# Attention layer of a macaron block: the next input's load, statistics and normalisation in other slots, and two reorderings on VectorE and on the DMA queue

## The reference

```
def attention(x, Wq, bq, Wkv, bkv, Wo, bo):            # 16 heads of 64
    q, k, v = split(x @ Wq + bq), split(x @ Wkv + bkv)
    q, k = rope(q), rope(k)                            # rotary positions
    probs = softmax(where(causal, q @ k.T / 8, -inf))  # 512 x 512 for each head
    return concat_heads(probs @ v) @ Wo + bo
```

## Time and profile before

| | us |
|---|---|
| median of 3 runs | 2536.84 (2534.6 to 2539.08) |
| the profiled execution | 2532.82 |
| its span, first to last instruction | 2530.7 |
| TensorE busy | 2345.7 (93%) |
| VectorE busy | 1879.8 (74%) |
| GpSimd busy | 1494.7 (59%) |
| ScalarE busy | 1467.9 (58%) |
| mean granted TensorE clock | 0.977 of full |

### The profile page before, as it was taken

One profiled execution on the slowest core, in us unless ns is written; L12 is line 12 of the kernel. 1 busy time (PEld: TensorE's weight loads), 2 busy tenths in 40 slices (PEclk: granted clock), 3 DMA queues, 4 the chain that ended last, 5 costly groups with the idle time before them and its releaser, 6 DMA issues. The chain is left out here.

```text
span 2530.7 us, 54615 instructions
## 1 busy us (share of the span) xinstructions
PE 2345.7 (93%) x17368; PEld 1820.5 (72%) x17368; DVE 1879.8 (74%) x3259; ACT 1467.9 (58%) x3733; POOL 1494.7 (59%) x1268
## 2 busy tenths in 40 slices
PE   7986899799999999999999999999999969976998
PEld 5753577578878888788788788888888846743676
DVE  6751377578888888898898888998888857731576
ACT  2321244377777777777777777777777723311343
POOL 1100255478888888888787888888888802100442
PEclk9998899999999999999999999999999989997999
DMA  7359664356565566566565665665665655559443
GB/s 252 117 208 391 246 196 157 99 150 177 163 178 167 161 182 172 162 179 170 151 189 157 173 174 165 168 181 156 177 175 163 177 152 190 205 235 380 135 150 104
DMA packets 336756, 460.86 MB, mean 182 GB/s; under 512 B 63200, under 2 KB 273760, under 8 KB 332384
## 3 DMA queue, kind: packets, MB, share of 16 engines
q1 hardware_dynamic: 336480, 457.47, 58.7%
HBM read 279.09 MB, written 111.15 MB: 154 GB/s over the span
## 5 line engine op out<-in xcount | busy, mean ns | idle before, releaser
L1374 POOL TENSOR_TENSOR att_z_sb<-att_z_sb,att_cos 128x512 f32<-128x512 f32 x255 | 347.9, 1364 | 222.4 <-DMA att_zs<-att_z_sb 222.2
L1585 ACT ACTIVATE att_prob<-att_ps_s,att_nmax 128x384 f32<-128x384 f32 (+2 forms) x768 | 356.5, 479 | 117.5 <-DVE att_nmax L1471 98.3
L1471 DVE TENSOR_REDUCE att_nmax<-att_ps_s 128x2 f32<-128x768 f32 (+3 forms) x512 | 410.3, 822 | 13.2
L1377 POOL TENSOR_TENSOR att_z_sb<-att_z_sb,att_zs 128x512 f32<-128x512 f32 x255 | 361.4, 1417 | 20.0
L1375 POOL TENSOR_TENSOR att_zs<-att_zs,att_sin 128x512 f32<-128x512 f32 x255 | 362.8, 1423 | 0.0
L1468 DVE TENSOR_TENSOR att_ps_s<-att_ps_s,att_masked 128x256 f32<-128x256 f32 (+1 forms) x384 | 195.5, 509 | 86.8 <-PE att_ps_s L1707 84.3
L1719 PE MATMUL att_ps_p<-sh_ident,att_prob 128*128 128x128 f32 x1536 | 236.7, 278 | 13.6 <-DVE att_probT L1485 13.4
L1585 ACT ACTIVATE att_last<-att_ps_s,att_nmax 128x512 f32<-128x512 f32 x256 | 173.9, 684 | 92.1 <-DVE att_nmax L1471 92.1
L1707 PE MATMUL att_ps_s<-att_kT_hi,att_qT_hi 64*128 64x256 f32 (+2 forms) x1024 | 194.0, 374 | 18.1 <-ACT att_prob L1585 14.6
L1733 PE MATMUL att_ps_p<-att_probT,att_v_sb 128*64 128x384 f32 (+2 forms) x1536 | 195.0, 389 | 6.7 <-DVE att_lastT L1490 6.7
L1719 PEld LDWEIGHTS att_ps_p<-sh_ident,att_prob 128*128 128x128 f32 x1536 | 170.5, 140 | 35.8 <-DVE att_probT L1485 17.7
(11 more groups left out here) (211 smaller groups left out, 6089.5 us busy)
## 6 DMA issues: line engine op xcount, KB each, us to landing
att_zs<-att_z_sb SPq DMA_DIRECT2D x512, 128.0 KB, 2.6
last_tile_blocks<-att_last SPq DMA_DIRECT2D x128, 512.0 KB, 3.0
att_got<-last_tile_blocks SPq DMA_DIRECT2D x512, 128.0 KB, 3.0
ffn_w<-in_e_W SPq DMA_DIRECT2D x56, 1024.0 KB, 13.5
att_R<-inverse_sums SPq DMA_DIRECT2D x256, 128.0 KB, 3.4
ffn_wg<-in_e_Wg SPq DMA_DIRECT2D x24, 1024.0 KB, 14.6
x_normalised_transposed<-dis_b_xnT SPq DMA_DIRECT2D x32, 512.0 KB, 2.8
dis_b_x<-in_x SPq DMA_DIRECT2D x16, 512.0 KB, 4.0
```

Source lines behind the costliest of these rows:

```text
L1374: nc.gpsimd.tensor_tensor(z[:, m, i, :], z[:, m, i, :], cos[:], ALU.mult)
L1377: nc.gpsimd.tensor_tensor(z[:, m, i, :], z[:, m, i, :], zs[:, m, i, :], ALU.add).then_inc(sum_s[i].sem, 1)
L1471: nc.vector.tensor_reduce(nmax[:, p % 2, qt, :], ps[:, :, at:at + (qt + 1) * P], AX.X, ALU.max, negate=True)\
L1585: nc.scalar.activation(dst, src, ACT.Exp, bias=nmax[:, p % 2, qt, hh:hh + 1], accum_out=sums[:, p % 2, hh, qt:qt + 1]).then_inc(exp_s.sem, 1)
```

## The change

- The residual's load goes from slot 0 of its own input to slot 7 of the input before (input 0 still loads its own in slot 0). A name BIAS = 0 keeps POOL's bias additions in slots 1 and 2.
- The next input's load goes from slot 1 to slot 0; the statistics from slot 2 (four tiles) to slots 1 and 2 (two tiles each). Moments stay in slot 3.
- `recentre` goes from the end of slot 3 to slot 4, behind `low_part` and ahead of `result`.
- `normalise` goes from slot 4's `exps` to: tiles 0 and 1 at the end of slot 4, tile 2 ahead of `exps` 2 and tile 3 ahead of `exps` 3 of slot 5.
- In slot 5 `turn` goes from ahead of `x_low` to the end of the slot, where it stands in all others; both `x_high` now stand ahead of `exps` 0.
- In every slot VectorE's `copy_pt` 1 goes from behind `largest` 2 to ahead of it.
- In every slot SP issues `rows` ahead of `get`.

```
-    XRES, X_LOAD, X_STATS, X_MOMENTS, X_NORM, X_TURN = 0, 1, 2, 3, 4, 5
+    XRES, BIAS, X_LOAD, X_STATS, X_MOMENTS, X_NORM, X_TURN = 7, 0, 0, 1, 3, 4, 5
...
                 if t.has(p - 1):
+                    rows(j, p - 1)
                     get(j, p - 1)
-                    rows(j, p - 1)
...
-                if p == XRES:
-                    need_held(sp, xo_s, j, 2 - NP)
+                if t.first and p == 0:
                     sp.dma_start(xres[:], tiles(x_dram, j)).then_inc(xres_in.sem, 16)
+                if p == XRES and not t.last:
+                    need_held(sp, xo_s, j, 2)
+                    sp.dma_start(xres[:], tiles(x_dram, j + 1)).then_inc(xres_in.sem, 16)
...
-                if p in (XRES + 1, XRES + 2):
+                if p in (BIAS + 1, BIAS + 2):
                     for i in range(2):
-                        residual(j, 2 * (p - XRES - 1) + i)
+                        residual(j, 2 * (p - BIAS - 1) + i)
...
                 if t.has(p - 2):
                     divide(j, p - 2)
+                if t.has(p - 1):
+                    copy_pt(j, p - 1, 1)
                 if t.has(p):
                     largest(j, p, 2)
-                if t.has(p - 1):
-                    copy_pt(j, p - 1, 1)
                 if t.has(p - 2):
                     low_part(j, p - 2)
-                if p == X_STATS and not t.last:
-                    statistics(j + 1, range(TT))
+                if p in (X_STATS, X_STATS + 1) and not t.last:
+                    statistics(j + 1, range(2 * (p - X_STATS), 2 * (p - X_STATS) + 2))
                 if p == X_MOMENTS and not t.last:
                     moments(j + 1)
+                if p == X_NORM and not t.last:
+                    recentre(j + 1)
...
                 if turning:
-                    turn(j, p - 1)
                     x_low(j + 1)
                 if t.output():
                     result(j, p - OUT0)
                 if t.has(p + 1):
                     query_low(j, p + 1)
-                if t.has(p - 1) and not turning:
+                if t.has(p - 1):
                     turn(j, p - 1)
-                if p == X_MOMENTS and not t.last:
-                    recentre(j + 1)
...
-                if norm:
-                    normalise(j + 1, (0,))
+                if turning:
+                    normalise(j + 1, (2,))
                 if t.has(p):
                     exps(j, p, 2)
-                if norm:
-                    normalise(j + 1, (1,))
+                if turning:
+                    normalise(j + 1, (3,))
                 if t.has(p):
                     exps(j, p, 3)
...
                 if turning:
                     x_high(j + 1, 0)
+                    x_high(j + 1, 1)
                 if t.has(p):
                     exps(j, p, 0)
                 if turning:
-                    x_high(j + 1, 1)
                     high(j, p + 1, 0)
                 if norm:
-                    normalise(j + 1, (2, 3))
+                    normalise(j + 1, (0, 1))
```

More of the change, by code:

```diff
@@ L1355, in slot @@
                     sp.dma_start(xin[:], tiles(x_dram, j + 1)).then_inc(x_in.sem, 16)
-                if t.first and p == XRES + 1:
+                if t.first and p == BIAS + 1:
                     for h in ffn_sems:
@@ L1400, in slot @@
                     key_low(j, p + 1)
-                if t.first and p == XRES:
+                if t.first and p == BIAS:
                     pool.wait_ge(bo_s, 1)
-                if p in (XRES + 1, XRES + 2):
+                if p in (BIAS + 1, BIAS + 2):
                     for i in range(2):
-                        residual(j, 2 * (p - XRES - 1) + i)
+                        residual(j, 2 * (p - BIAS - 1) + i)
             pool.wait_ge(rope_in, 16 * 16)
```

## The result

The changed kernel takes 2522.82 us (median of 6 runs, 2518.74 to 2527.38), the kernel before in the same comparison 2537.99 us (6 runs, 2534.6 to 2539.96). The ratio is 0.9943 with a 95% interval of 0.9929 to 0.9958: 15.2 us, or 0.6%, faster. The forecast was 2515.0 with a range of 2506 to 2530. The direction and the range held; the gain was 6.6 us smaller than forecast. The profiled execution took 2521.39 us, span 2519.3.

The account below looks back on a forecast made before the run. TensorE (PE) was taken to bound ordinary slots. Terms 12 + 5.4 + 1 + 1.7 + 1.7 = 21.8 us off the profiled 2532.82 gave 2511.0; adding 4.0 to reach the runs' median gave 2515.0, range 2506 to 2530.

Parts of the forecast that it names:

- The copy ahead of the third mask: Slot 6: PE's wait for VectorE's copy of `transposes` 1 goes; 12 us gained, 6 at worst, 13.4 at best.
- The same 0.5 us elsewhere: Other slots: VectorE's later steps move back 0.5 us, covered by 1.2 of slack in slots 0, 7 and 3; zero cost.
- Net +1, from -2 to +2: Slots 1 and 2, statistics split: slot 2 0.8 less, 0.5 more; slot 1 1.3 more against 1.2 cover; 1 us gained.
- Recentre in slot 4: Slot 4: waits of 8.3 us and up to 2.1 in input 0 go, 5 charged for `recentre` ahead of `result`; 5.4 gained.
- The charge of 0.33 us an input: Slot 4: `recentre` makes `result` 0.53 us late for PE, less about 0.2 absorbed by held `low_part`; 5 us over 15.
- Recentre is short: Rival, 0.18: in slot 4 `recentre` lasts only what is left of POOL's operation; 5 us more gained, 2510.0.
- Rows ahead of get: SP queue: freed 1.5 us or more earlier each slot, helping PE only in input 0; 1.7 us gained, 0 to 2.4.
- Slot 5: Slot 5: `turn` no longer precedes `x_low`; of 5.6 us of PE waits 1.7 gained, from 0 to 3.
- Result becomes the bound: Rival, 0.20: VectorE's late `low_part` and full-length `recentre` take back most; 8.3 us gained, 2528.5.
- the new wait for `result` at 15 us or more on PE: Sign the forecast is wrong: PE's k projection waits that long for `result`; some 5 us would show it right.
- Slower: Rival, 0.06: `low_part`, started 0.5 later, waits for all of POOL's next operation; 19 us slower, 2556.

Follow-up runs that it names:

- the copy alone: The kernel before with only `copy_pt` 1 moved ahead of the third mask (`largest` 2) in every slot: 2532.22 us against 2539.45, ratio 0.9972.
- the copy back: The changed kernel with `copy_pt` 1 again behind the third mask (`largest` 2): 2519.97 us, ratio 0.9927 to the kernel before.
- `rows` alone: The kernel before with SP issuing `rows` ahead of `get` and nothing else: 2536.7 us against 2536.74, ratio 0.9999.
- the two versions that wait less: The changed kernel with the copy early in slot 6 only (2513.33 us, 0.9904), and that with `recentre` also moved to POOL (2509.92 us, 0.9898).

## Why the prediction was right, and where it was too high

**The copy ahead of the third mask.** Right in its working: slot 6 fell by 0.55 us of the 0.76. The prediction said that `low_part`, held by POOL, would not move, with 0.1 to spare. In the kernel before it ends at 8.22 to 8.28 us of the slot in ten of 14 inputs; in the changed kernel at 8.36 to 8.39 in eight, and there the slot is 10.6; in the others it met POOL's next operation, and the slot is up to 11.30 long. That gave 7.7 us in inputs 1 to 14 and 0.7 in input 0; with the 1.0 us of input 15 it is 9.4, where the prediction took 12 between 6 and 13.4. That input 15's part comes from the copy is not shown: with the copy alone that input took 1.3 us more than before.

**The same 0.5 us elsewhere, and the statistics.** The shift was right (0.59 us: `low_part` starts at 7.68 of a slot instead of 7.08), and zero in slots 0, 3 and 7 was right. The failed step is "Net +1, from -2 to +2" for slots 1 and 2: measured -5.5 us (14 x 0.26 and 14 x 0.13), outside its ends. It set the mean idle time, 0.76, against a mean cost, and 0.76 is the mean of the 79 slots that had such idle time; 33 had none. But `low_part` lasts anything from 0.68 to 1.8, so the cover is gone in some inputs whatever the mean: slot 1 is 11.7 where `low_part` is 0.7 to 1.2 long and 12.0 to 12.4 where it is 1.4 to 1.7. With the copy back, the split statistics give back what the prediction expected of them: 11.71 and 11.75.

**Recentre in slot 4.** The gain was right: the wait for `exps` (8.3 us) is gone. The charge of 0.33 us an input was the other mis-sized term: measured 0.65 (12.35 against 11.70), so inputs 1 to 14 gained nothing in slot 4 (-0.3 us in sum). The prediction took 0.2 off, as a held `low_part` would absorb part of the shift; in slot 4 it absorbed 0.06 (1.21 long in the mean, against 1.27 with the copy back). The rival *Recentre is short*, 5 us more by the rule from the Trainium skill, did not come about, though the runs bear the rule out: `low_part` directly ahead also needs both inputs from SBUF, POOL's next operation is drawn 0.39 to 0.52 us ahead of `recentre` in all 15 cases, and so `recentre` waits for all of it (1.23 to 1.25). The short cases appeared once `result` stood between the two. The 15 long cases of the kernel before, which the prediction held against that rival, were of this kind as well: there POOL's L1374 is drawn 0.06 to 0.21 us ahead of `recentre` each time.

**Rows ahead of get, and input 0.** Taken at 1.7 us, and 2.1 for input 0's wait in slot 4; measured 4.0 in slot 3 and 3.2 in slot 4, of which 3.2 and 2.4 come with `rows` alone. Mis-sized: the prediction counted PE's named wait for the turned tile (2.4 us) and not that in the same slots POOL waits 2.5 us for its swapped halves from this queue, and ScalarE 2.5 us for POOL. SP's wait for the sums fell from 203.3 us to 3.3, and for inputs 1 to 14 nobody gained by it, as foreseen; that `get` comes later, which the prediction charged nothing for, costs 3.4 us where `turn` still precedes `x_low`, and nothing in the changed kernel.

**Slot 5.** 14.68 to 14.54: 1.9 us, taken at 1.7. `x_low` now starts 9.81 to 9.91 us into the slot, before 9.74 to 10.69. The normalisations cost nothing there, as foreseen.

**The sum.** 9.4 - 5.5 + 2.9 (slot 4 with input 0) + 4.0 + 1.9 + 1.2 for the shorter stall at the loop's end, which varies from trace to trace, is 13.9 us, against 13.8 by which the stage is shorter in the two traces; the medians differ by 15.2. The rival *Result becomes the bound* (0.20, 2528.5) described the mechanism that in fact set the slots, but input 0 gave 7.2 us in slots 3 and 4, where the forecast had 3.8. Its sign of recognition, the new wait for `result` at 15 us or more on PE, lay between: 9.7 us on PE and 27.6 on the weight loads. So the number came nearer to the forecast than its working deserves: without the 3.4 us too little for input 0 and the 1.2 of the stall, for neither of which the prediction had a term, the sum is 9.3 us, near that rival's 8.3 and not the forecast's 21.8. It would still lie in the range. In the rival *Slower*, the sum has a + 4 that its own words, "with the copy term gone", leave without a source.

## What to carry to other kernels

Where an order of steps is repaired for one slot, repair it for that slot alone: the copy ahead of the mask was worth 0.56 us where nothing else filled the time, and cost 1.0 us over three other slots where it made the engine wait. Cover that is held against a cost must be compared case by case, not by its mean, when an operation in front of it varies from 0.68 to 1.8 us. A tiny operation is not cheap by its size: put it on the engine that made its input, or behind an operation that does not compete with GpSimd, and not directly behind a long one that does.

## What the runs showed of the hardware that was not expected

- A short VectorE operation directly behind a long one, both with two SBUF inputs, waits for a whole POOL operation. 128x4 numbers took 1.23 to 1.25 us behind `low_part` in 15 of 15 cases, 0.15 to 1.24 behind an operation on PSUM, and 0.15 to 0.28 with POOL's operations shortened. It is no strict alternation: `query_low` directly behind `recentre` took 0.68 in 12 of 15 cases, with POOL's operation held to 1.8, and 1.79 in the three where POOL's was drawn ahead of it.
- A `low_part` that POOL holds ends at a fixed distance behind POOL's operation: 0.546 to 0.554 us in the 84 cases of the changed kernel that took over 0.75. Free, it takes 0.68; held, up to 1.82.
- POOL's own records include its waiting: 1.74 us instead of 1.29 where it was held by `low_part`.
- PE's weight loads show a late producer sooner than its matmuls do: in inputs 1 to 14 they wait 27.6 us for `result`, the matmuls 9.7, and by the slots without the stall those inputs were 12 to 16 us longer than in the two versions that wait less (96.69 against 95.80 and 95.55; weight loads 13.9 and 9.5 us).
